# Two edits at the end of a linear attention: three small reductions behind an offset on VectorE, sixteen unread products on TensorE

## The reference

```python
x = x + jnp.tanh(g_xattn[0]) * _L0_xattn_ref(_layernorm(x), ctx, ctx)      # linear attention
x = x + jnp.tanh(g_ffn[0]) * _L0_ffn_ref(_layernorm(x), codes, absmax, lora) # 4-bit weights + low rank
...
# _L0_xattn_ref: 8 heads
qh = softmax(qh, axis=3); kh = softmax(kh, axis=1)
kvs = einsum('bnhd,bnhe->bhde', kh, vh); out = einsum('bnhd,bhde->bnhe', qh, kvs)
# _L0_ffn_ref
Wg = dequant4(g_codes, g_absmax).T        # likewise Wu, Wd
y1 = x1 @ Wg + x1 @ g_lora_a @ g_lora_b   # likewise y2
y3 = (relu(y1) * y2) @ Wd + ...
```

## Time and profile before

| | |
|---|---|
| median of 3 timed runs | 1976.78 us (1976.6 to 1978.18) |
| the profiled execution | 1977.45 us, its span 1975.7 us |
| TensorE busy | 1923.7 us, 97% |
| VectorE, ScalarE, GpSimd busy | 64%, 63%, 42% |
| mean granted TensorE clock | 0.995 of full speed |

### The profile page before, as it was taken

The page is one execution under the profiler, slowest core; times in us unless marked ns, Lnnn a source line. Parts: engine busy times, 40 slices in busy tenths (PEclk is TensorE's granted clock), DMA queues, the critical chain, the costliest instruction groups (busy, mean ns, idle before and its releaser), DMA issues. The chain is left out here.

```text
span 1975.7 us, 26472 instructions
## 1 busy us (share of the span) xinstructions
PE 1923.7 (97%) x9188; PEld 969.1 (49%) x9188; DVE 1271.2 (64%) x2185; ACT 1248.6 (63%) x1990; POOL 821.4 (42%) x746
## 2 busy tenths in 40 slices
PE   7997999999999999999999999999998899999998
PEld 6774444444444444444444444444444455555544
DVE  6786676573645647365463745546389988888872
ACT  6895888767867777776777767766534434344331
POOL 3433744531323232232322323222278767767742
PEclk9998999999999999999999999999999999999999
DMA  6641733258566373755737465562551010111001
GB/s 222 232 139 53 252 97 111 88 181 285 185 219 234 121 269 107 248 203 167 259 103 268 147 221 202 159 243 82 204 165 32 33 54 27 44 54 41 24 22 43
DMA packets 90117, 288.33 MB, mean 146 GB/s; under 512 B 11777, under 2 KB 16641, under 8 KB 73089
## 3 DMA queue, kind: packets, MB, share of 16 engines
q1 hardware_dynamic: 89984, 286.64, 43.2%
HBM read 259.33 MB, written 27.26 MB: 145 GB/s over the span
## 5 line engine op out<-in xcount | busy, mean ns | idle before, releaser
L1207 ACT ACTIVATE first<-first 128x512 f32<-128x512 int32 x1016 | 631.0, 626 | 34.3 <-DMA first<-in_codes 8.2
L1432 POOL TENSOR_TENSOR gu<-wt,gu 128x512 f16<-128x512 f32 x82 | 97.5, 1189 | 378.9 <-ACT gu L1228 378.9
L1605 DVE SCALAR_TENSOR_TENSOR wt<-first,w_scale,absm 128x512 f32<-128x512 f32 x128 | 99.9, 781 | 240.3 <-ACT first L1207 240.3
L1940 PE MATMUL a_psQ<-z,gu 128*128 128x512 f16 x840 | 187.2, 379 | 0.0
L2539 PE MATMUL a_psL<-z,l_x 128*128 128x512 f16 x768 | 170.7, 379 | 0.8 <-DVE l_x L2641 0.8
L1940 PE MATMUL a_psC<-z,gu 128*128 128x512 f16 x660 | 151.3, 379 | 0.0
L1940 PE MATMUL a_psC<-z 128*128 128x512 f16 x612 | 140.4, 379 | 0.0
L1940 PEld LDWEIGHTS a_psQ<-z,gu 128*128 128x128 f16 x840 | 82.2, 98 | 99.1
L1432 POOL TENSOR_TENSOR dn_lo<-wt,dn_hi 128x512 f16<-128x512 f32 x42 | 49.5, 1178 | 189.9 <-ACT dn_hi L1228 189.9
L1444 POOL TENSOR_TENSOR hid_lo<-z,hid_hi 128x512 f16<-128x512 f32 x68 | 81.0, 1205 | 109.6 <-ACT hid_hi L1269 109.5
L1608 DVE SCALAR_TENSOR_TENSOR wt<-a_psE,lora_gain,wt 128x512 f32<-128x512 f32 x128 | 96.1, 751 | 44.9 <-PE a_psE L1898 21.0
(11 more groups left out here) (441 smaller groups left out, 4197.6 us busy)
## 6 DMA issues: line engine op xcount, KB each, us to landing
z<-x_parts SPq DMA_DIRECT2D x126, 1024.0 KB, 6.1
first<-in_codes SPq DMA_DIRECT2D x132, 256.0 KB, 3.0
absm<-in_absmax SPq DMA_DIRECT2D x264, 128.0 KB, 3.3
c_in<-in_ctx SPq DMA_DIRECT2D x16, 512.0 KB, 5.5
X<-in_x SPq DMA_DIRECT2D x16, 512.0 KB, 4.4
gu<-in_ctxT SPq DMA_DIRECT2D x16, 512.0 KB, 3.5
o_sp<-in_w SPq DMA_DIRECT2D x16, 512.0 KB, 4.7
z<-in_ctx SPq DMA_DIRECT2D x8, 1024.0 KB, 7.2
```

What stands on the lines that cost most here:

```text
L1207: act.activation(level[w % 2][:], codes[w % RING] if k == 0 else level[w % 2][:], ACT.Prelu, bias=bias, scale=scale, alpha=alpha).then_inc ...
L1432: pool.tensor_tensor(low, source, high, ALU.subtract).then_inc(wlo_done, 1)
L1605: dve.scalar_tensor_tensor(wt[at], source[:], w_scale[:, m:m + 1], absm[w % RING][:], ALU.mult, ALU.mult).then_inc(scaled, 1)
L1940: mm = pe.matmul(out, w[:, k * P:(k + 1) * P], xx[:, k], start=first and q == 0, stop=q == 3 * KD // 2 - 1, skip_group_check=True)
```

## The change

VectorE's "own" part moves behind the offset of step 15. TensorE gets, in step 17 ahead of the wait for the last normalised tile, sixteen matmuls of 128 x 512 into psQ, whose results nobody reads; L384 overwrites them.

```diff
@@ tensor, step, behind the transposes of psB @@
+                    if i == TILES + 1:
+                        pe.wait_ge(turned_done, TILES)
+                        for n in range(16):
+                            pe.matmul(res["psQ"][:, n % 2, :].rearrange("p (q t) -> p q t", q=QUARTS), x_tiles(res, 0)[:, 0, 0, 0, 0, n % 4],
+                                      x_tiles(res, 0)[:, 0, 0, :, 0, n % 4], start=True, stop=True)
                     if exists(i - 2):
                         pe.wait_ge(xn_done, i - 1)
@@ vector, step @@
                     if i == TILES - 3:
                         scales_dve(dve, "rows")
-                    if i == TILES - 1:
-                        scales_dve(dve, "own")
                     if exists(i - 1):
                         offset(i - 1, 1 - h, mv2, rstd2, nmr2, rstd2_done, nmr2_done)
                     if exists(i + 2):
                         prepare(i + 2, h)
                     if i == TILES - 1:
+                        scales_dve(dve, "own")
                         scales_dve(dve, "top")
                         scales_dve(dve, "every")
```

## The result

The changed kernel takes 1980.28 us (median of 20 runs, 1979.38 to 1982.64), the kernel before 1977.81 (20 runs, 1976.6 to 1979.13). The ratio is 1.0015, interval [1.0009, 1.0021]: slower by 1.8 to 4.2 us; the medians themselves are 2.5 us apart. That is about the 0.2% named as the bound of what one measurement tells, but clear over this many runs. The forecast was 1977.5 in a range up to 1979.1. Size and range were wrong: the loss is about 2.5 us where +0.7 was forecast. The profiled execution has 1981.1 us, span 1979.4. The ratios leave out one execution of the kernel with the move alone, which took 3403 us at a mean granted clock of 0.557.

What follows compares the result with a forecast made beforehand. TensorE, at 97% of the span, was taken as the bound. Products starting +0.94 us late, between half and all lost, gave +0.7: 1978.15 for the profiled execution, 1977.5 us against the timed median of 1976.78; range 1975.0 to 1979.1.

Steps and rivals of the forecast that it cites:

- The offset gains nothing from the move: VectorE, offset of step 15 at 158.77 us: cannot start sooner, blocked again for 2.29 us by GpSimd's multiplication; gain 0.
- The small reductions lose their cover, +0.94: VectorE's L233 to L235 behind the offset: L216's 2.6 us of cover goes, so L238 and the 48 products come 0.94 us later.
- The sixteen products don't hold the clock: TensorE's pause before tile 15's transposes: clock taken low again for the first of the 48; gain 0, other bound 2.5 us.
- the fall at 1487.1: Nearest profile row: clock fell after a pause of 1.59 us; used to argue the clock would fall here too.
- The first rival: The clock holds through the pauses before the 48 products: -2.5 + 0.94 = -1.5 us, 1975.3; chance 0.15.
- They hold nothing up: The sixteen run from 167.7 to 171.2 us, leaving 2.4 us of pause before 173.56; cost 0.
- the third rival: The sixteen run at the low clock and hold up the last tile, if ending after 174.7: +1.9 us, 1978.7; chance 0.08.
- Of the late start half is lost, 0.7 in sum: The 48 products start 0.94 us late; all or half (0.47) is lost, depending on the clock's rise; middle taken, +0.7 us.
- Their end moves the whole rest of the kernel by as much: The 48 products L384 close the first block, whose end every engine waits for, so later work shifts equally.
- cost 0 for the products: The sixteen added products in TensorE's pause: psQ unread until L384, semaphore long reached, nothing held up; cost 0.
- the 0.05 for what I didn't see: Remaining chance, 0.05, for the unseen, such as another state of the queues at the block's start.

Runs made afterwards that it cites:

- the fill alone: Kernel before plus 20 products of 512 columns in the long pause, six and three behind rank products, reductions ahead of the offset: 1976.53 us against 1977.44, ratio 0.9997.
- 16 narrow products: Kernel before plus sixteen unread products of 2 columns instead of 512, reductions left ahead of the offset: 1979.06 us, ratio 1.0007.
- second profile of before: The kernel before, unchanged, profiled once more: 1977.31 us, ratio 0.9999.

## Why the prediction was wrong

**The offset gains nothing from the move: right.** 2.29 us at 158.83, behind the multiplication's start by 0.07.

**The small reductions lose their cover, +0.94: right as a mechanism, and in size where the clock was up** (0.92 with the move alone). In the profile of the changed kernel it was 1.41, since the clock fell in the pause of 3.42 us that the move opened. I had given L216 and L220 the high clock's lengths without asking what the longer pause can do to them.

**The sixteen products don't hold the clock: right, with luck in the reason.** It was low again from 174, ahead of the transposes. The row that I leaned on, the fall at 1487.1 behind a pause of 1.59 us, decides nothing: behind the same pause of 1.59 us the clock stayed up with the fill alone and with 16 narrow products. The first rival and the rule of the Trainium skill that stands with the prediction ("TensorE: Matmul & The Clock Gate", section "HAM oscillation — how this bites in real kernels") would have it that a pause cut to 2.4 us keeps the clock. It was cut to 2.34 us and the clock fell. With 29 products and no pause over 1.6 us it held and gave 2.3 us, so filling pays here, in a larger dose. **They hold nothing up: right**, 2.34 us of pause remained. (The limit of 174.7 in the third rival is a slip: 176.57 - 1.76 - 0.6 is 174.2. The sixteen ended at 171.8, so nothing hangs on it. Likewise 1978.7 and 0.3 give 1979.0, not 1979.1.)

**Of the late start half is lost, 0.7 in sum: right for the move alone** (0.94 on the chain, block end +0.72), **too small for the change.** There the 48 started 1.43 us late and ended 1.27 late: only 0.16 came back, since the rise moved too, from 183.2 to 184.3.

**"Their end moves the whole rest of the kernel by as much", and cost 0 for the products: the step that failed.** 0.8 us are lost behind the block's end, in code that the change doesn't touch, to an instruction fetch that 32 more instructions shift onto SyncE's first loads. That is 12.06 against 11.25 us (11.49 in the second profile of before), and it appears with products of 2 columns and goes with 128 of them. I had counted the engines' time of the sixteen and not their code.

The sum by the profiles is 1.27 + 0.81 = 2.1 us; the medians say 2.5, with 1.8 to 4.2 as the interval. Against the second profile of before, which is slower in both places, the same sum is 0.9 + 0.6 = 1.5 us, counted from the end of GpSimd's power. So the two terms are of the right kind and each is known to some tenths of a microsecond only. The difference may be the clock near 1549 or nothing. None of the rivals had this case; it sat in the 0.05 for what I didn't see, which did name the state of the queues at the block's start.

## What to carry to other kernels

Unread products that are to keep TensorE's clock up should bridge every thin stretch up to the work that profits: 29 in three pauses did so here and saved 2.3 us, sixteen in one pause did not. An added instruction takes room in the code as well as time: after any such edit look at the first loads of the next block, and at where the instruction fetch falls. And a stall that looks like slack under an instruction may be the cover of what stands ahead of it: ask what is queued behind the stalled one before moving work there.

## What the runs showed of the hardware

- A 16 KB instruction fetch that begins shortly ahead of an absmax issue lengthens it: in the kernel before eight issues take 1.08 to 1.58 us instead of 0.47 or 0.60, each ending 0.37 to 0.38 us behind the fetch's packet. At the second block's start the pair takes 1.71 to 2.69 us instead of 1.11. The fetch's place was the same again with 256 added instructions.
- Codes whose issue is followed by a fetch within 2 us land later: 3.71 us behind their issue in the median of 12 loads of the kernel before, 2.99 without a fetch near (96 loads). How a fetch holds them back is not shown.
- A product of 2 columns costs TensorE 0.03 us (128 of them in 3.35 us).
- Letting a VectorE instruction past GpSimd's multiplication can move the stall to another: with the offset through in 0.16 us, L240 took 1.35 us in its place (0.22 elsewhere). The three reductions between them took 0.17 to 0.21 us.
- The same program reaches the changed place at different times: GpSimd's power of step 15 ends at 157.94 to 160.02 us in the fourteen profiles, whose kernels are the same up to there, and the clock's first rise comes at 14.5 to 18.5 us (15.95 and 16.93 in the two profiles of the kernel before). A difference of a microsecond between two profiles has to be counted from a common event.
